# The order of four engines around the last batch's routing and the first experts of a transformer block on one core

## The reference

```
x = layernorm(x + attention(x))          # 16 heads of 64, softmax over 1024 keys
x = layernorm(x + memory(ctx, x))        # concatenation of moved rows of x, ctx and a strided conv of x
x = layernorm(x + switch_ffn(x))         # 8 experts, top-1, capacity 128 tokens per batch and expert
# switch_ffn, for each batch:
logits = x @ Wg;  gates = softmax(logits);  expert = argmax(gates)
pos = number of earlier tokens of the batch with the same expert;  keep = pos < 128
y[token] = gate * (gelu(x[token] @ W1[expert]) @ W2[expert])     # 0 where not kept
```

## Time and profile before

| | |
|---|---|
| median of 3 runs | 1908.08 us (1907.01 to 1909.49) |
| the profiled execution | 1907.01 us, span 1905.2 us, so 1.8 us lie around the span |
| TensorE | busy 1841.5 us, 97% of the span |
| VectorE | busy 1223.7 us, 64% |
| ScalarE | busy 859.1 us, 45% |
| GpSimd | busy 1344.2 us, 71% |
| TensorE on the chain that ended last | 83% of the span |

### The profile page before, as it was taken

The page is one execution under the profiler, slowest core; times in us unless marked ns, Lnnn a source line. Parts: engine busy times, 40 slices in busy tenths (PEclk is TensorE's granted clock), DMA queues, the critical chain, the costliest instruction groups (busy, mean ns, idle before and its releaser), DMA issues.

```text
span 1905.2 us, 30739 instructions
## 1 busy us (share of the span) xinstructions
PE 1841.5 (97%) x11400; PEld 1175.7 (62%) x11400; DVE 1223.7 (64%) x2147; ACT 859.1 (45%) x1101; POOL 1344.2 (71%) x719
## 2 busy tenths in 40 slices
PE   7899999999999999999999999999999998999998
PEld 5555555555665565556666565556665554598887
DVE  5466655666766657756666657666666667765565
ACT  3344444444435443344345533343444543465674
POOL 1688787778666867697678767797668676662564
PEclk9899999999999999999999999999999999999999
DMA  4210000002312000022211000021111011444340
GB/s 139 85 40 18 23 18 23 18 23 74 99 29 62 23 18 23 23 64 88 78 44 41 18 23 7 32 81 56 45 44 37 17 34 34 153 125 134 128 133 34
DMA packets 132142, 104.24 MB, mean 55 GB/s; under 512 B 58140, under 2 KB 118684, under 8 KB 130972
## 3 DMA queue, kind: packets, MB, share of 16 engines
q1 hardware_dynamic: 128924, 93.81, 16.6%
q0 software_dynamic: 3072, 8.46, 1.2%
HBM read 69.15 MB, written 29.43 MB: 52 GB/s over the span
## 4 chain that ended last, share of the span: by engine, by line
PE 83%; DVE 5%; POOL 5%; issue 3%; ACT 2%; DMA 1%; SPq 0%; POOLq 0%; DVEq 0%; ACTq 0%
PE score_ps L1127 23%; PE av_ps L1141 21%; PE spare_ps L1090 9%; PE spare_ps L1106 8%; PE spare_ps L1083 5%; PE spare_ps L441 4%; PE y_ps L1704 3%; PE h_ps L1675 3%; PE spare_ps L1152 3%; POOL prob_sum L1011 3%; DVE max_of L1283 1%; PE spare_ps L490 1%; PE spare_ps L465 1%; POOL expert_rows L430 1%; POOL wp_lo L1437 1%
## 5 line engine op out<-in xcount | busy, mean ns | idle before, releaser
L1011 POOL TENSOR_TENSOR prob_sum<-prob_sum,probs 128x1024 f32<-128x1024 f32 (+1 forms) x384 | 905.8, 2359 | 202.6 <-ACT probs L1227 170.6
L1283 DVE TENSOR_REDUCE max_of<-spare_ps 128x1 f32<-128x512 f32 x1024 | 656.6, 682 | 346.5 <-PE spare_ps L1106 335.6
L1227 ACT ACTIVATE probs<-score_ps 128x1024 f32<-128x1024 f32 x512 | 502.8, 1025 | 686.6 <-PE score_ps L1127 671.5
L1141 PE MATMUL av_ps<-probs,v 128*64 128x512 f32 x2048 | 488.0, 602 | 3.0 <-ACT probs L1227 1.6
L1141 PEld LDWEIGHTS av_ps<-probs,v 128*64 128x64 f32 x2048 | 129.8, 136 | 241.6 <-issue 221.1
L1007 POOL TENSOR_TENSOR prob_sum<-probs 128x1024 f32<-128x1024 f32 (+1 forms) x64 | 150.2, 2347 | 146.9 <-ACT probs L1227 146.8
L1106 PE MATMUL spare_ps<-k_hi,q_hi 64*128 64x512 f32 x1024 | 230.6, 443 | 21.9 <-DVE max_of L1283 21.1
L1106 PEld LDWEIGHTS spare_ps<-k_hi,q_hi 64*128 64x128 f32 x1024 | 99.6, 185 | 224.6 <-issue 189.2
L1127 PE MATMUL score_ps<-q_hi,k_hi 64*128 64x512 f32 x1024 | 211.7, 407 | 1.1 <-DVE o_in L1333 0.9
L1127 PE MATMUL score_ps<-shift_rows,ones 64*128 64x512 f32 x1024 | 205.7, 395 | 0.0
L1127 PE MATMUL score_ps<-q_lo,k_hi 64*128 64x512 f32 x1024 | 205.4, 394 | 0.0
(11 more groups left out here) (249 smaller groups left out, 2367.7 us busy)
## 6 DMA issues: line engine op xcount, KB each, us to landing
o_transposed<-o_out SPq DMA_DIRECT2D x64, 256.0 KB, 2.0
v<-in_L_ffn_W_dram SPq DMA_DIRECT2D x16, 1024.0 KB, 6.0
o_in<-o_transposed SPq DMA_DIRECT2D x28, 512.0 KB, 4.1
w_raw<-in_L_attn_Wq_dram SPq DMA_DIRECT2D x64, 64.0 KB, 2.3
w_raw<-in_L_attn_Wk_dram SPq DMA_DIRECT2D x64, 64.0 KB, 2.2
wv_raw<-in_L_attn_Wv_dram SPq DMA_DIRECT2D x32, 128.0 KB, 2.8
shift_rows<-neg_rows SPq DMA_DIRECT2D x256, 1.0 KB
x<-in_x_dram SPq DMA_DIRECT2D x4, 1024.0 KB, 5.9
```

What stands on the lines that cost most here:

```text
L1011: pool.tensor_tensor(out, out, probs[:, n % RING, heads], ALU.add).then_inc(prob_added, 1)
L1141: last = pe.matmul(av_ps[hd * E:(hd + 1) * E, :], v[:, quad % 2, kt, 2 * first_head + hd, :], probs[:, n % RING, hd, :], start=(kt == 0), ...
L1227: act.activation(probs[:, n % RING], score_ps[n % 2][:, :, :], ACT.Exp).then_inc(probs_ready, 1)
L1283: dve.tensor_reduce(max_of[:, u % 2, kh, j, hd:hd + 1], bank[:, :], AX.X, ALU.max).then_inc(pass_read, 1)
```

## The change

The diff moves instructions in the lists of four engines and changes two banks. In the part of TensorE the lines left out are the transposes of the four pairs and the score products, in the part of VectorE `find_kept` to `find_rows`:

```diff
-        x2T_bank = [xeT_ps[:, g % KC, :] for g in range(TB // 2)]
+        x2T_bank = [y_bank[1 + g % 2] for g in range(TB // 2)]
@@ GpSimd: def _(pool)
-            for c in range(HC):
+            for c in range(6):
                 h_low(pool, 0, c)
             weights.split_low(pool, 0, 1)
+            for c in range(6, HC):
+                h_low(pool, 0, c)
             weights.split_low(pool, 1, 1)
@@ TensorE: def _(pe)
             def transpose_rows(g):
                 wait(pe, xeT_done, g)
+                if g == 1:
+                    pe.wait_ge(route.old_placed, b + 1)
+                    pe.wait_ge(route.comp_added, b + 1)
...
             up(0, range(6, HC))
+            transpose_rows(1)
             pe.wait_ge(gelu_done, 6)
             down_begins(0)
-            down(0, range(B - 1), range(6))
-            pe.wait_ge(route.old_placed, b + 1)
-            pe.wait_ge(route.comp_added, b + 1)
+            down(0, [0], range(6))
...
-            transpose_rows(1)
-            down(0, range(B - 1), range(6, HC))
-            up(1, range(1))
+            down(0, [1], range(6))
             pe.wait_ge(route.logits_out, TB // 2 * (b + 1))
             route.count(pe, b, late_bank)
-            up(1, range(1, HC))
+            down(0, [2], range(6))
+            down(0, range(B - 1), range(6, HC))
+            up(1, range(HC))
@@ ScalarE: def _(act)
-            for c in range(HC):
+            for c in range(6):
                 gelu(0, c)
             route.load_table(act, ACT.Sqrt)
+            split_w1(1)
             route.take_root(act, 1, b)
             route.norm2(act, b, range(HT, TB))
             for g in range(0, TB // 2, 2):
                 route.x2T_out(act, b, g, x2T_bank[g])
-            split_w1(1)
             rows_high(1)
+            for c in range(6, HC):
+                gelu(0, c)
+            route.exp_gates(act, b)
             split_w2(1)
-            route.exp_gates(act, b)
@@ VectorE: def _(dve)
             route.choose(dve, b)
+            route.count_masks(dve, b)
             rows_low(1)
-            route.count_masks(dve, b)
...
             for c in range(2):
                 h_low(dve, 1, c)
-            add_gated(0)
-            for c in range(2, 4):
-                h_low(dve, 1, c)
-            find_moments(0)
-            for c in range(4, HC):
+            add_rows(0)
+            for c in range(2, HC):
                 h_low(dve, 1, c)
             norm(0)
+            add_rows(1)
             rows_low(LATE)
-            add_rows(1)
```

More of the change, by code:

```diff
@@ L1889, in add_rows @@
             def add_rows(p, tiles=None):
-                add_gated(p, tiles)
-                find_moments(p, tiles)
-            def add_gated(p, tiles=None):
                 e, t0, t1 = PASSES[p]
+                tiles = tiles or range(t0, t1)
                 wait_sent(dve, e - 2)
-                for t in tiles or range(t0, t1):
+                for t in tiles:
                     dve.wait_ge(y_ready, TILES_TO[p] + t - t0 + 1)
@@ L1901, in add_gated @@
                                              ).then_inc(z_done, 1)
-            def find_moments(p, tiles=None):
-                e, t0, t1 = PASSES[p]
-                tiles = tiles or range(t0, t1)
                 for t in tiles:
```

## The result

The changed kernel takes 1919.35 us (median of 5 runs, 1918.55 to 1922.2) against 1908.08 for the kernel before: a ratio of 1.0058, with a 95% interval of 1.0044 to 1.0074. It is 11.3 us slower (8.4 to 14.1). The forecast was 1911.0, with a range up to 1915.5, so the sign of the sum was right and its size was not.

A forecast was written before the change was run, and what follows sets the result against it. TensorE, busy 97% of the span, was taken as the bound, with up_late's start at 1733.20 deciding. A start 1.55 us late plus 1.3 for low clock gave +2.9 us: 1911.0 against 1908.1, range 1907.0 to 1915.5.

The forecast's parts named there:

- the last term: In up_late: lower clock after the new wait makes its products slower, +1.3 us, bounds 0 and 1.7.
- the first term: Late transposes and down(1) ahead of up_late: a shorter wait for late data, ending at 1732.15, a gain of 1.05 us.
- The wait for `rows_low(LATE)`: Ahead of up_late: rows_low(LATE) now stands behind add_rows(1) on VectorE, a new uncovered wait of 2.6 us.
- The gain ahead of it: Late transposes and the 30 down products end at 1732.15, a gain of 1.05 us before the new wait.
- The hold of GpSimd's split: At the norm of x2: GpSimd's weight split delays VectorE, first pair 1.5 us late, TensorE idle 3.45 us.
- The low clock through the scores: Rival, chance 0.30: 32 scores take 7 us instead of 3.5 after the idle time; total about +6, 1914 us.
- The rivals in which the routing comes out early: VectorE not held at the norm: 1908 us, chance 0.15; row numbers not held by GpSimd's second split either: 1906, chance 0.07.
- the forecast's row: At the scores: the earlier profile's higher clock after the x2 transposes is assumed again, so scores take 3.5 us.

The follow-up runs named there:

- the 20 products in the wait: Kernel before with only rows_low(LATE) moved behind add_rows(1), plus 20 unused 256-column products in the wait ahead of up_late: 1911.33 us, ratio 1.0011.
- The version with the one line undone: Changed kernel with rows_low(LATE) put back ahead of add_rows(1): 1906.08 us, ratio 0.9993 to the kernel before.
- the changed kernel's second profile: Changed kernel run again with nothing altered, for a second profile: 1923.27 us, ratio 1.0081 to the kernel before.
- the one traced execution: Kernel before with rows_low(LATE) behind add_rows(1) and 8 unused products ahead of up_late: traced execution 1909.1 us, median 1918.04, ratio 1.0064.

## Why the prediction was wrong, step by step

**The step that failed** is the last term: "in `up_late` that is 1.3 us, with bounds 0 and 1.7". It took the length of the slow stretch from places where mostly products of 256 columns or more follow, 3.4 and 2.8 us, and put it on a place where 96 products of 128 columns follow. There the clock did not come back before they were over. Measured: 18.7 instead of 10.67 in `up_late` and about 1.8 more for the eight transposes and the first `down` products behind it, so 9.8 us in place of 1.3. By time, the 20 products in the wait took back 9.7. With that one term the sum is -1.05 + 2.6 + 9.8 = 11.35, against 11.3 measured. That it fits to the tenth is luck: the first term isn't shown (below), and the changed kernel measured again was 14.0 us slower. The upper bound was not a bound: the nearest rows were of another product shape, and it should have been all of `up_late` at the price of the lower clock, some 10 us (20.47 us in one profile).

**The wait for `rows_low(LATE)`** was right: 2.6 forecast, 2.47 in the profiles, 2.1 by time.

**The gain ahead of it** is not shown. 1.05 us were forecast for the late transposes and `down(1)`. The version with the one line undone has 41.8 us from the group 1 transposes to `up_late`, where the prediction has 42.0 (1732.15 - 1690.19) and the kernel before has 43.0. But the same stretch, without the new wait, took 44.1 us in the changed kernel's second profile and 44.9 in that with 20 products ahead of `up_late`, and in the five profiles with TensorE's order of before it took 42.7 to 45.8 (from the first product of `down(0)`): the spread is larger than the gain. By time the version with the one line undone is 2.2 us under its kernel before, but the interval reaches past 1. One part of the account was off: 1.4 us of waiting for the late tiles were forecast, and neither profile of the changed kernel waits there, since TensorE itself comes later. The count came 16.8 us after the group 1 transposes in its second profile, against 16.9 forecast.

**The hold of GpSimd's split** was right: 3.07 us of wait against 3.45 forecast, L506 in 2.41 against 2.6 (from 1694.4 to 1697.05). The Trainium skill (SBUF — State Buffer, SBUF: two separate sides) describes the port that VectorE and GpSimd share as a lock that one holds for a whole instruction; the 2.41 us beside the split and the 1.38 without it agree.

**The low clock through the scores**, the rival with 0.30, came about in some executions. The 32 scores took 6.83 us in the changed kernel's first profile and 6.84 in that with 20 products ahead of `up_late`, and 3.7 to 3.9 in its second and in that of the one line undone; the window 1700.62 to 1704.30 has a granted clock of 0.96. Where it came, it cost what the rival said, about 3 us (6 instead of 2.9). The profile with the 20 products and that with the one line undone have the same waits of 0.4 and 0.7 us behind the count, and 44.9 against 41.8 us from the group 1 transposes to the end of `down(1)`:

```profile
1688.40 0.82 PE L1658 MATMUL xeT_ps<-ident,probs 128*128 128x128 f32 x6
...
1697.79 6.84 PE L490 MATMUL y_ps<-wg,x 128*128 128x8 f32 x32
...
1733.28 2.56 PE L1717 MATMUL y_ps<-w_hi,h_hi 128*128 128x256 f32 x20
```

How many of the executions without a trace had slow scores is open. The Trainium skill (TensorE: Matmul & The Clock Gate, Part 4: PE-mode transpose) says that transposes don't count as busy like products. The traces don't decide on it: in the changed kernel's second profile the clock was 0.50 over the last of the 16 transposes and back up in the scores right behind them, and in its first profile it was up over a part of the transposes (0.74 over all) and down through all scores. So the forecast's row, scores at the higher clock, did not always hold either.

**The rivals in which the routing comes out early** are gone: VectorE was held at the norm in every profile with the new order on GpSimd, and the first x2 transpose came 6.0 us after the group 1 transposes, against 6.2 forecast.

## What to carry to other kernels

A short wait of TensorE can cost far more than its length. Here 2.47 us ahead of 96 products of 128 columns cost 11.8 us. Look at what follows the wait, and price all of it at the lower clock as the bound. The cheapest cure is order (an instruction that another engine waits for goes ahead of a block that only its own result needs). Where order can't be changed, 20 unused products of 256 columns in the wait gave back 8 to 9 us here. When several edits go together, one small one can be all of the cost: one line undone turned 1919.4 us into 1906.1. And a sum that meets the measured time to the tenth proves none of its terms: look for each in more than one profile.

## What the runs showed of the hardware that I had not expected

The clock did not fall during the wait of 2.47 us but behind it, in the middle of steady products: about 2 us behind it in three profiles, 0.6 us in the changed kernel's second, and almost at once in that with 26 products ahead of the x2 transposes. In all five it then stayed at 0.50 over the 128-column products that followed, up to 20.47 us of them, while the same 96 products, begun at the higher clock without a wait ahead, took 10.67 us at 1.00. So one and the same list of products has two durations. The length of the wait alone did not settle which: 1.95 us was followed by the lower clock in one profile and 1.98 us was not in another, and a wait of 1.46 us was followed by a fast `up_late` in the one traced execution and, as their times suggest, by a slow one in the five others.
